# Splitting k's norms from q's, all of attention's sums ahead of layer 3's second chunk, layer 3's odd chunks in other banks, and an order of its own for the first image

## The reference

```python
def layer0(x):                                   # attention, three convolutions, residual
    q, k, v = split(affine(x) @ w_qkv + b_qkv)   # N = 4096 tokens x 48
    q, k = q - mean(q, channels), k - mean(k, channels)
    q2 = l2n(q*q / (sum(q*q, channels) + 1e-7), channels)
    k2 = l2n(k*k / (sum(k*k, channels) + 1e-7), tokens)
    kv = einsum('nc,nd->cd', k2, v)
    attn = (v + q2 @ kv / sqrt(N)) @ w_ln + b_ln
    y = concat([attn, x], channels)              # 96 channels
    y = leaky_relu(conv1x1(y, w1) + b1, 0.2)
    y = leaky_relu(conv3x3(y, w2) + b2, 0.2)
    return conv1x1(y, w3) + b3 + x

def layer1(x):                                   # layer 3 is the same, with the same weights' shapes
    y = depthwise3x3(relu(x), dw) + dw_bias
    return affine(y @ pw + pw_bias)

def layer2(x):                                   # weights mixed by a router, 48 -> 192 -> 48
    rw = sigmoid(mean(x, pixels) @ Wr + br)      # four experts
    h = relu(bn1(x @ mix(rw, Wpw) + rw @ bpw))
    h = relu(bn2(depthwise3x3(h, mix(rw, Wdw)) + rw @ bdw))
    return bn3(h @ mix(rw, Wpwl) + rw @ bpwl) + x

def reference(x):
    return layer3(layer2(layer1(layer0(x))))
```

## Time and profile before

| | |
|---|---|
| median of three runs | 1086.94 us |
| the profiled execution's own time | 1086.49 us |
| its span in the trace | 1084.7 us |
| mean granted TensorE clock | 0.966 |
| PE busy | 993.6 us, 92% of the span |
| DVE busy | 874.8 us, 81% |
| ACT busy | 473.2 us, 44% |
| POOL busy | 96.0 us, 9% |
| the chain that ended last, by engine | PE 59%, DVE 18%, issue 11%, SP's queue 5%, DMA 4%, ACT 3% |
| one pass of the loop | 122.9 us, six times |

### The profile page before, as it was taken

How to read it: one execution, slowest core, us unless ns; L and a number is a source line. 1 busy time by engine, 2 the same in 40 slices (tenths; PEclk the granted TensorE clock), 3 DMA queues, 4 the chain that set the end, 5 groups by cost and what they waited for, 6 DMA issues and landing times.

```text
span 1084.7 us, 14728 instructions
## 1 busy us (share of the span) xinstructions
PE 993.6 (92%) x4598; PEld 634.8 (59%) x4598; DVE 874.8 (81%) x1207; ACT 473.2 (44%) x813; POOL 96.0 (9%) x120
## 2 busy tenths in 40 slices
PE   4689869999999989999999989999999989988986
PEld 3456656665665565665665566655755666654634
DVE  6662478998599968999599968999599968998970
ACT  3311425355533636355533636354543646334522
POOL 0210013001200003001200013001110013000000
PEclk9799969999999999999999999999999999999999
DMA  5242814195435555284434645275443845235314
GB/s 71 49 122 55 133 31 131 36 151 108 109 80 84 114 113 142 44 134 107 109 97 74 124 105 148 45 123 109 104 110 64 134 105 133 56 79 119 72 27 103
DMA packets 129520, 104.48 MB, mean 96 GB/s; under 512 B 97903, under 2 KB 98772, under 8 KB 129492
## 3 DMA queue, kind: packets, MB, share of 16 engines
q1 hardware_dynamic: 129492, 104.14, 46.7%
...
## 4 chain that ended last, share of the span: by engine, by line
PE 59%; DVE 18%; issue 11%; SPq 5%; DMA 4%; ACT 3%; POOL 0%; DVEq 0%; ACTq 0%; POOLq 0%
PE bank L1269 25%; DVE dwa L696 7%; PE bank L1301 7%; PE bank L1249 5%; PE bank L1275 4%; DMA y_parts<-a_parts 3%; PE bank L1316 3%; DVE s L618 2%; PE bank L1317 2%; SPq L979 2%; PE bank L1241 2%; PE bank L1285 2%; PE bank L1304 2%; PE bank L1303 2%; DVE a_parts L789 2%
## 5 line engine op out<-in xcount | busy, mean ns | idle before, releaser
L696 DVE SCALAR_TENSOR_TENSOR dwa<-h1a,dyn,dwa 128x1024 f32<-128x1024 f32 x224 | 280.9, 1277 | 1.0
L1269 PE MATMUL bank<-y_parts,w_l 128*96 128x512 f32 x576 | 151.3, 407 | 0.0
L1269 PE MATMUL bank<-y_parts,w_h 128*96 128x512 f32 x576 | 147.0, 399 | 0.0
L696 DVE SCALAR_TENSOR_TENSOR dwb<-h1b,dyn,dwb 128x1024 f32<-128x1024 f32 x112 | 142.9, 1276 | 0.5
L1301 PE MATMUL bank<-a_parts,wt_h 128*112 128x512 f32 x384 | 122.1, 427 | 22.5 <-DMA y_parts<-a_parts 19.4
L1269 PEld LDWEIGHTS bank<-y_parts,w_l 128*96 128x96 f32 x576 | 91.6, 163 | 61.2 <-issue 21.3
L1269 PEld LDWEIGHTS bank<-y_parts,w_h 128*96 128x96 f32 x576 | 93.0, 162 | 43.8
L1301 PEld LDWEIGHTS bank<-a_parts,wt_h 128*112 128x112 f32 x384 | 65.9, 181 | 58.1 <-issue 35.2
L1128 POOL TENSOR_TENSOR y_low<-y,y_parts 96x512 fp32r<-96x512 f32 x56 | 67.1, 1199 | 237.3 <-DVE y L750 237.3
L1121 POOL TENSOR_TENSOR tok<-tok,u 128x1536 f32<-128x1536 f32 x8 | 24.3, 3036 | 579.9 <-DVE u L620 579.9
L1249 PE MATMUL bank<-xq,w_cur 97*96 97x512 f32 x128 | 67.9, 612 | 3.7 <-DVE y L750 3.7
...
## 6 DMA issues: line engine op xcount, KB each, us to landing
...
a_parts<-a_parts SPq DMA_DIRECT2D x128, 66.0 KB, 2.5
...
```

Source lines behind the costliest of these rows:

```text
L696: nc.vector.scalar_tensor_tensor(out=dst, in0=tap_input(n, t), scalar=weight, in1=dst, op0=ALU.mult, op1=ALU.add).then_inc(tap_step, 1)
L1269: nc.tensor.matmul(bank[0:C2, :], wgt[:, t, :], y1_parts[:, part, rows, cols], start=part + t == 0, stop=False)
```

## The change

There are seven parts.

1. **k's norms first.** `norms_begin` sums only k's squares, and the new `norms_of_q_begin` does the same for q later: in the loop behind the low part of layer 3's chunk 2. The semaphore `u_ready` counts two per image; POOL waits for the first.
2. **Sums in one piece.** In the loop PE does all 64 matmuls of `attention_sums` ahead of layer 3's chunk 1. Before, 32 stood ahead of it and 32 behind that chunk and the first output transposes.
3. **The mean from two tensors.** `mean_b` is written by a `SCALAR_TENSOR_TENSOR` (ones x mean x ones) in the place of a `TENSOR_SCALAR`, and the factor 1/TOKENS moves to the router's sum, which becomes a `SCALAR_TENSOR_TENSOR` as well. `gs` is a tensor of its own and no view of `routed` any more.
4. **Layer 3 in other banks.** The odd chunks of layer 3 go to banks 4 and 5. They wait there for the high part of their own chunk, and not for ACT's eviction of the chunk before. Conv1's first two chunks in these banks now wait for layer 3's evictions, and so do the last image's taps on PE in bank 4.
5. **Taps ahead of a low part.** The last place of `steps_at` (11 taps) is split into 4, which stand ahead of the low part of layer 3's chunk 1, and 7.
6. **ACT's order.** In the loop ACT evicts the transposes of x and the first half of the scores ahead of the projection's second chunk.
7. **The first iteration's own order.** With no `back`, PE does all scores ahead of layer 1's chunks 2 and 3, and the sums ahead of the routing; DVE brings the sums back and does q's norms before it mixes the weights; ACT takes the fourth powers before the sigmoid.

The diff:

```diff
...
         routed = sb("routed", [P2, M])
-        wk, mean_b, gs = routed[0:C2, :], routed[:, 0:128], routed[:, 0:SUMS]
+        wk, mean_b = routed[0:C2, :], routed[:, 0:128]
+        gs = sb("gs", [P2, SUMS])
...
-        D_P, D_L3, D_OUT = 0, (4, 5, 7, 9), (6, 8, 10, 11)
+        D_P, D_L3, D_OUT = 0, {0: 4, 2: 6}, (5, 7, 8, 9)
         ring_d = Ring(banks[6:8], [(ah3_ready, PCHUNKS, n + 1) for n in range(PCHUNKS)]
-                      + [(outc_ready, PCHUNKS, 1), (outc_ready, PCHUNKS, 2), (ot_ready, 4, 1), (outc_ready, PCHUNKS, 3),
-                         (ot_ready, 4, 2), (outc_ready, PCHUNKS, 4), (ot_ready, 4, 3), (ot_ready, 4, 4)], first_free=True)
+                      + [(outc_ready, PCHUNKS, 1), (ot_ready, 4, 1), (outc_ready, PCHUNKS, 3),
+                         (ot_ready, 4, 2), (ot_ready, 4, 3), (ot_ready, 4, 4)], first_free=True)
+        def l3_bank(m):
+            return banks[4 + m // 2] if m % 2 else ring_d.bank(D_L3[m])
...
         BY_CONV1, BY_CONV2, BY_PROJECT = 0, CHUNKS, 2 * CHUNKS
-        steps_at = (0,) * CHUNKS + (6, 3, 3, 4, 3, 4, 3, 3) + (2, 3, 2, 3, 11)
+        steps_at = (0,) * CHUNKS + (6, 3, 3, 4, 3, 4, 3, 3) + (2, 3, 2, 3, 4, 7)
...
                 dve.wait_ge(squared, 16 * image + 16)
-                attn_chain(nc.vector.tensor_reduce(s1[:, :, :], tokens(Q_AT, [[K_AT - Q_AT, 2]]), axis=AX.X, op=ALU.add))
-                attn_chain(nc.vector.tensor_scalar_add(s1[:, :, :], s1[:, :, :], 1e-7))
-                nc.vector.reciprocal(u[:, :, :], s1[:, :, :]).then_inc(u_ready, 1)
+                sums_of_squares(image, 1, K_AT)
+            def sums_of_squares(image, part, at):
+                attn_chain(nc.vector.tensor_reduce(s1[:, part, :], tokens(at), axis=AX.X, op=ALU.add))
+                attn_chain(nc.vector.tensor_scalar_add(s1[:, part, :], s1[:, part, :], 1e-7))
+                nc.vector.reciprocal(u[:, part, :], s1[:, part, :]).then_inc(u_ready, 1)
+            def norms_of_q_begin(image):
+                sums_of_squares(image, 0, Q_AT)
             def norms_of_q(image):
                 dve.wait_ge(q4_ready, image + 1)
-                dve.wait_ge(u_ready, image + 1)
+                dve.wait_ge(u_ready, 2 * image + 2)
...
                 dve.wait_ge(mean_sum, f + 1)
-                nc.vector.tensor_scalar(mean_b[:, :], ones[0:P2, :], mean[:, 0:1], 1.0 / TOKENS, ALU.mult, ALU.mult)\
-                    .then_inc(mean_ready, 1)
+                nc.vector.scalar_tensor_tensor(out=mean_b[:, :], in0=ones[0:P2, :], scalar=mean[:, 0:1], in1=ones[0:P2, :],
+                                               op0=ALU.mult, op1=ALU.mult).then_inc(mean_ready, 1)
             def route(f):
                 dve.wait_ge(rw_done, f + 1)
-                nc.vector.tensor_tensor(rwz[:, :], ring_b.bank(B_RW)[:, 0:EXPERTS], br[:, :], ALU.add).then_inc(rwz_ready, 1)
+                nc.vector.scalar_tensor_tensor(out=rwz[:, :], in0=ring_b.bank(B_RW)[:, 0:EXPERTS], scalar=1.0 / TOKENS, in1=br[:, :],
+                                               op0=ALU.mult, op1=ALU.add).then_inc(rwz_ready, 1)
...
                 if back is not None:
+                    depthwise_at(back, BY_PROJECT + 4)
                     l3_low_part(back, 1)
-                    depthwise_at(back, BY_PROJECT + 4)
+                    depthwise_at(back, BY_PROJECT + 5)
                 else:
...
                     l3_low_part(back, 2)
+                norms_of_q_begin(attn)
                 mean_out(f)
...
                 x2_low_part(f, 3)
-                route(f)
-                mix_weights(f)
-                mix_project(f)
-                project_weights()
-                norms_of_q(attn)
-                sums_apart(attn)
-                norms_end(attn)
-                sums_out(attn)
+                if back is None:
+                    sums_apart(attn)
+                    route(f)
+                    sums_out(attn)
+                    norms_of_q(attn)
+                    mix_weights(f)
+                    mix_project(f)
+                    project_weights()
+                    norms_end(attn)
+                else:
+                    route(f)
+                    mix_weights(f)
+                    mix_project(f)
+                    project_weights()
+                    norms_of_q(attn)
+                    sums_apart(attn)
+                    norms_end(attn)
+                    sums_out(attn)
...
             norms_begin(0)
+            norms_of_q_begin(0)
...
                 pool.wait_ge(squared, 16 * image + 16)
-                pool.wait_ge(u_ready, image + 1)
+                pool.wait_ge(u_ready, 2 * image + 1)
...
                         bank = ring_c.take(pe, image, C_1 + k - 1)
+                        if f is not None and k <= 2:
+                            after(pe, outc_ready, PCHUNKS * (f - 1) + 2 * k)
...
                 for m in chunks:
-                    if layer == L3 and image is LAST - 1 and m == 0:
-                        pe.wait_ge(ah3_ready, PCHUNKS * image + 1)
-                        bank = ring.bank(places[m])
+                    if layer == L3 and (m % 2 or image is LAST - 1 and m == 0):
+                        pe.wait_ge(ah3_ready, PCHUNKS * image + m + 1)
+                        bank = l3_bank(m)
...
                     n, b = PE_CHUNKS[nth], PE_BANKS[nth]
+                    if b == 4:
+                        pe.wait_ge(outc_ready, PCHUNKS * (LAST - 1) + 2)
...
                 transpose_x(attn, range(4))
-                attention_scores(attn, range(4))
-                l1(f, (2,))
-                attention_scores(attn, range(4, 8))
-                l1(f, (3,))
-                if back is not None:
+                if back is not None:
+                    attention_scores(attn, range(4))
+                    l1(f, (2,))
+                    attention_scores(attn, range(4, 8))
+                    l1(f, (3,))
                     project(back, (2, 3))
                     l3(back, (0,))
-                routing(f)
-                attention_sums(attn, range(RUN // 2))
-                if back is not None:
+                    routing(f)
+                    attention_sums(attn, range(RUN))
                     l3(back, (1,))
                     out_tokens(back, (0,))
-                attention_sums(attn, range(RUN // 2, RUN))
-                if back is not None:
                     l3(back, (2,))
+                else:
+                    attention_scores(attn, range(8))
+                    l1(f, (2, 3))
+                    attention_sums(attn, range(RUN))
+                    routing(f)
+                if back is not None:
...
                     act.wait_ge(l3_done, PCHUNKS * b + m + 1)
-                    nc.scalar.activation(outc_of(b)[:, m * BANK:(m + 1) * BANK], ring_d.bank(D_L3[m])[0:P2, :], ACT.Identity,
+                    nc.scalar.activation(outc_of(b)[:, m * BANK:(m + 1) * BANK], l3_bank(m)[0:P2, :], ACT.Identity,
...
                 l1_out(f, (1,))
+                x_out(attn, range(4))
+                scores_out(attn, range(4))
                 if back is not None:
                     project_affine(back, f + 1, 1)
-                x_out(attn, range(4))
-                scores_out(attn, range(8))
+                scores_out(attn, range(4, 8))
...
                     project_affine(back, f + 1, 3)
+                if back is None:
+                    fourth_powers(attn)
                 route(f)
-                fourth_powers(attn)
-                if back is not None:
+                if back is not None:
+                    fourth_powers(attn)
...
```

11 lines of the change are left out of this document (6 added, 5 removed).

## The result

The changed kernel's median is 1069.67 us over four runs (1068.44 to 1070.61), against 1086.7 us of the kernel before (1084.78 to 1086.99): a ratio of 0.9854 with a 95% interval of 0.984 to 0.9867. The forecast was 1067.8 us. The profiled execution took 1068.75 us, its span is 1066.9 us, and the mean granted clock 0.975 in the place of 0.966.

A forecast was written before the change was run, and what follows sets the result against it. DVE and SP, then PE, were taken to bound each pass. Passes -12.0, start -1.9, first iteration -4.6 and last -0.7 sum to -19.2 us, giving 1067.8 us, with 8 in 10 between 1052 and 1075.

The forecast's parts named there:

- Rival A: Chunk 2's low part on DVE gets in before POOL's product of k: 4.4 us a pass, 1053.5 us in all; chance 0.18.
- one tie: DVE's low part of chunk 2 and POOL's product of k start within 0.02 us and exclude each other; POOL taken to win.
- The six passes: Loop: chunk 3 of layer 3 starts 2.0 us earlier in each pass, -12.0 us for the six.
- The last iteration: Two waits for ACT's eviction ahead of layer 3's chunks go: -0.7 us.
- The start and the first iteration: k's product starts earlier on POOL: -1.9 us; scores and sums come earlier in the first iteration: -4.6 us.
- the likeliest case: Whole kernel: POOL wins and the low part is held; 1067.8 us, own range 1063 to 1071, chance 0.62.
- T0 + 2.43 for POOL's start: T0 ends a pass's last tap on DVE; k's reciprocal was forecast at about T0 + 2.35, POOL's start at about 622.03.
- idle ahead of the routing: PE, behind chunk 0, waits about 1.0 us for the mean, a gap that did not exist before.
- The wait ahead of chunk 2: PE waits 0.4 us ahead of layer 3's chunk 2 for its copies.
- Rival C: The clock falls to 1.2 GHz behind waits of 1.0 and 1.05 us: 1.0 a pass lost, 1073.8 us; chance 0.12.
- the price put on the old gap: About 1.5 us a pass lost to the slow clock behind PE's old gap of 2.38 us ahead of chunk 1.
- this loss: In each pass POOL's product holds chunk 2's low part on DVE, which ends 1.05 us later than before.

The follow-up runs named there:

- sums_split: The changed kernel with half of attention's sums moved back behind layer 3's chunk 1 and its output transposes, in the passes; 1078.71 us.
- banks_in_turn: The changed kernel with layer 3's odd chunks in ring D's banks in turn again, so chunks 2 and 3 wait for ACT's evictions; 1072.55 us.
- mean_one_tensor: The changed kernel with the mean's product by TENSOR_SCALAR from one tensor and the factor 1/TOKENS there again; 1069.14 us.
- first_as_before: The changed kernel with the first iteration in its old order on PE, DVE and ACT, k's norms still first; 1073.0 us.
- before_k_first: The kernel before with only k's norms first and q's norms behind the low part of layer 3's chunk 2; 1083.25 us.
- acts_taps_loop: The changed kernel with parts 5 and 6 undone in the loop alone, the last iteration's order kept; 1068.32 us.
- low_first: The changed kernel, but from image 2 on POOL's product of k also waits for the low part of layer 3's chunk 2; 1057.6 us.
- pool_halves: The changed kernel with POOL's product of k as two instructions of half the size; 1061.55 us.
- acts_taps_as_before: The changed kernel with ACT's old order around the projection's second chunk and DVE's 11 taps unsplit, which also changed the last iteration's taps; 1075.33 us.
- Part 2 alone: The kernel before with only all of attention's sums ahead of layer 3's chunk 1 in the loop; 1070.43 us.

## Why the prediction was right

**Which case it was.** Rival A and the forecast were the two ways of one tie, and the trace has both: five passes with the low part held (3.33 to 3.35), one with POOL held. The chance was given to the kernel as a whole, though the tie is decided anew in each pass, and it is far from even: in seven other traces that leave it open (sums_split, banks_in_turn, mean_one_tensor, first_as_before, both acts_taps runs and before_k_first) POOL came first in all 42 passes. The four runs of the changed kernel lie in two pairs 2 us apart (1068.44 and 1068.75; 1070.60 and 1070.61). Why is not shown: only one of them has a trace, and mean_one_tensor and acts_taps_loop, with no such pass in their traces, are as fast (1069.14 and 1068.32). The runs low_first and pool_halves show that the hold is what these passes lose by: decide it, or halve the instruction, and the time follows.

**Where it was right by luck.** The span fell by 17.7 us where 19.2 were forecast, and the terms met that less well than the sum. The six passes gave 12.3 for the 12.0 forecast, but 2.4 of them are the one tie that went the other way; without it they would have given 9.9. The last iteration lost 1.1 us where 0.7 was to be gained. The start and the first iteration gave their 6.5. So a tie that the likeliest case did not hold made up for one of two misses of about 2 us each.

**The pass.** T0 + 2.43 for POOL's start, 2.80 for its product, 1.02 idle ahead of the routing, 0.90 (forecast 1.05) ahead of chunk 1, full clock there, no wait ahead of chunk 3: the steps are as written. The sum was 2.0 us a pass and the traces have 1.7 to 1.9 in the passes 2 to 5. The wait ahead of chunk 2 was the undersized term: 0.44 to 0.75 in place of 0.4, ended by the copies in three of these passes and by ACT's eviction in the one shown. A slip of 0.05 in the working (1.75, 0.35 and 0.2 add to 2.30, not to 2.35) did no harm: the reciprocal ended 2.34 behind T0.

**What was left out of the sum.** The first pass gained 0.9 only. PE stood 1.48 ahead of chunk 2 there, behind one issue of L1011 on SP that took 1.76 in place of 0.60. This is the piece in the chain of waits, ahead of it one of the usual length:

```profile
256.89 0.60 SPq L1011
...
257.86 1.76 SPq L1011
```

That this issue alone made the wait is not shown. In low_first, too, it was slow in the first pass (1.39, a wait of 2.25), but in acts_taps_as_before PE waited 1.50 at the same place without a slow issue, behind a copy that took 4.25 us where the one of the second pass took 3.69. Why the first pass is the slow one stays open.

**Start and first iteration.** 1.9 + 4.6 = 6.5 was forecast; the first T0 in the loop came at 244.01 in place of 250.54, 6.53 earlier. That the two agree so closely is chance: six other traces with the same start and first iteration have this T0 between 243.18 and 245.09. How the gain divides between the parts is known roughly. With k first alone T0 came 4.1 earlier (246.46, before_k_first) or 2.4 (248.19, first_as_before), and part 7 brought the rest.

**The last iteration.** The forecast was -0.7; from its first conv2 matmul to the end it took 172.1 us (from 894.79) in place of 171.0 (from 913.66). Two runs whose last iteration has the same order took 170.0 (mean_one_tensor) and 169.7 (acts_taps_loop), so the forecast was near and the changed kernel's execution lost some 2 us. The rows put this down to the clock. The three go alike, within 0.2 us, to a gap of 3.21 us (L1399, 76 us behind the start), which the kernel before has too. Then the granted clock is at the 1.2 GHz level for 10.2 us, from 972.3, in the changed kernel and for 3.4 us in the other two, and L1377 follows 106.62 us behind the start in the place of 104.76 and 104.62. Why the clock stayed down longer there, no run shows. The two waits of 0.48 for ACT, ahead of chunks 2 and 3, went; one of 0.61 for the copies stands ahead of chunk 2 in the changed kernel's trace, and none in the other two.

**The clock.** Rival C, a fall behind two gaps of 1 us, did not come in any pass of the loop. But the price put on the old gap was right only as far as the kernel before fell every time.

**Which part did it.** Part 2 alone gives 0.9845, as much as all seven together. In the changed kernel parts 4 and 7 are worth about 3 us each, part 1 some 3 in the start and the first iteration, and in the loop it takes 5.8 back; part 3 gives nothing, nor do parts 5 and 6 in the loop. The parts don't add up exactly, since each fills a wait that another one would have filled. The prediction named these terms, but it had them in one sum and did not say that part 1 in the loop should be left out. The likeliest case held this loss (1.05 us a pass for the low part) without drawing the consequence.

The Trainium skill's rule in "SBUF — State Buffer", section "Who interferes with whom", was what put the low part's hold into the sum. The rows agree with it in all three points used: two SBUF inputs are held (3.33), a reduction isn't (L627 at 853.78, 1.75 beside POOL's product), and the hold ends with the instruction (2.03 with half the product).
